# Mamba layer with a 16-state scan: the sum over the states as accumulating transposes

## The chip, the cores and the metric

One core of one Trainium2 chip. The metric is the device time in microseconds; three runs of the kernel before took 5519.04, 5524.55 and 5525.06 us, median 5524.55.

## The reference, cut to what matters

Two layers on x of shape (2, 512, 64, 64), each added to its input behind a group norm. Layer 0 is a Mamba block over 4096 tokens, 1024 inner channels and 16 states; layer 1 is linear attention with 8 heads. The change is in layer 0's scan:

```python
def step(h, inp):
    u_t, d_t, b_t, c_t = inp
    dA = jnp.exp(d_t[..., None] * A)
    dBu = (d_t * u_t)[..., None] * b_t[:, None, :]
    h = dA * h + dBu
    y = jnp.einsum('bdn,bn->bd', h, c_t)      # the sum over the 16 states
    return (h, y)
...
y = ys.transpose(1, 0, 2) + u * D_skip
y = y * jax.nn.silu(z)
out = y @ out_proj_w.T
```

## The kernel before, in words

All is f32. Layer 0 is cut into 16 chunks of 512 tokens (2 images x 8). A chunk has 8 tiles of 128 inner channels (j), a tile has 16 states (n), so a chunk has 128 slots, slot = 16 j + n. Every engine walks through the same slots in order, in a function of its own (scalar_chunk, vector_chunk, gpsimd_chunk, tensor_chunk, sync_chunk), and a table of slot numbers (lines 29 to 41) says in which slot it does what else. The loop over chunks runs with the scan of chunk c, the front part (norm, input projection, convolution, delta) of chunk c + 1, and the output projection of chunk c - 1 at once. Chunks 1 to 14 are one hardware loop (line 340), so each engine turns back 13 times.

A state (n) of a tile (j) goes through four engines:

- ScalarE, line 501: exp(delta * A) into one of three PSUM banks, two slots ahead; line 482: the last column of the previous scan is kept as the carry.
- VectorE, line 586: the product delta * u * B into one of eight hs buffers, one slot ahead; line 591: the scan.
- GpSimd, line 625: hc = h * C into one of four hc buffers, as soon as TensorE is done with the sum four states before (line 624).
- TensorE, line 718: y_ps += hc, a product with the identity as the weights and hc as the moving 128x512 operand, two slots behind (SUM_LAG). y_ps is one PSUM bank. The first of the 16 waits for y_skip (line 717), the last step's read of that bank.

Behind a tile's last sum, VectorE adds the skip term in slot 3 of the next tile (line 559, Y_SKIP), GpSimd multiplies with silu(z) in slot 5 (line 620, Y_GATE). In the same slots TensorE has the z products of the tile (line 692, slots 2, 2, 2, 3), the input products of the next chunk (line 660, four per inner tile, in slots 42 + 8 t to 45 + 8 t) and the output products of the chunk before (line 708). ScalarE has the group norm of the next chunk (line 398, slots 4, 5, 9, 10, the first waits for the load of xn), the copy of an input product out of PSUM (line 429, six slots behind its first part) with the last tap (line 435), and softplus (lines 457 to 472), whose Ln in slot 6 (10 for the last tile) brings a table load before it and one behind it. VectorE has the convolution (line 538). Each engine works strictly in the order of its code, so a wait holds up all that is behind it on that engine.

In layer 1 (from line 751) the same TensorE does plain f32 products of 128x128 (line 1047) and f32 transposes of 128x128 by the identity (line 1074).

```python
pe.wait_ge(hc_ready, step - SUM_LAG + 1)
if ns == 0:
    wait(pe, y_skip, tile)
pe.matmul(y_ps[:, :], identity[:, :], hc[:, ns % HC_RING, :], start=ns == 0,
          stop=ns == STATE - 1).then_inc(n_summed, 1)
```

Of the kernel before, what the change touches and what calls it, by code (L numbers as in the profile page):

```python
# [8 lines left out]
ACT = mybir.ActivationFunctionType  # L9
AX = mybir.AxisListType  # L10

P = 128
BATCH, DIM, TOKENS = 2, 512, 4096
CT = DIM // P
T = 512
CB = TOKENS // T
CHUNKS = BATCH * CB
INNER, STATE, TAPS, RANK = 1024, 16, 4, 32
# [4 lines left out]
GN_EPS = 1e-5  # L23
H_RING, HC_RING, DA_RING = 8, 4, 3
SUM_LAG = 2

# [9 lines left out]
DT_MM, SP_ABS, SP_EXP, SP_ROUND, SP_LN, SP_REST, SP_SUM, SP_DELTA = 14, 1, 3, 4, 6, 7, 9, 10  # L38
DT_MM7, SP_ABS7, SP_EXP7, SP_ROUND7, SP_LN7, SP_REST7, SP_SUM7, SP_DELTA7 = 3, 6, 7, 8, 9, 10, 11, 12
Z_MM, Z_TANH, Z_SILU = (2, 2, 2, 3), 8, 11  # L40
Y_SKIP, Y_GATE = 3, 5


def wait(engine, sem, value):

    if isinstance(value, int) and value <= 0:
        return
    engine.wait_ge(sem, value)
# [60 lines left out]
def mamba_and_linear_attention(nc, x, ln_w, ln_b, in_proj, conv_w, conv_b, x_proj, dt_proj, dt_b, a_log, d_skip,  # L109
# [9 lines left out]
    with outer:  # L119
# [3 lines left out]
        def sem(name):  # L123
            return outer.enter_context(nc.semaphore(name))

        identity = sb("identity", [P, P])
# [4 lines left out]
        with layer0:  # L131
# [30 lines left out]
            sp_l = sb("sp_l", [P, T], layer0)  # L162
# [3 lines left out]
            hc = sb("hc", [P, HC_RING, T], layer0)  # L166
# [4 lines left out]
            y_ps, da_ps = banks[0], banks[1:4]  # L171
# [139 lines left out]
            sp_sum = sem("sp_sum")  # L311
# [7 lines left out]
            h_ready = sem("h_ready")  # L319
            hc_ready = sem("hc_ready")  # L320
            n_summed = sem("n_summed")
            y_skip = sem("y_skip")
            gated = sem("gated")
            out_mm = sem("out_mm")
# [21 lines left out]
            with ExitStack() as main:  # L346
# [35 lines left out]
                def scalar_chunk(act, c, scan, front, project):  # L382
                    f = c + 1
                    for j in range(JT):
                        for n in range(STATE):
                            tile, slot = JT * c + j, STATE * j + n
# [63 lines left out]
                            if front if j == 7 else scan:  # L450
                                nt = tile + 1
                                dt_ps = pout if j == 7 else pb
                                jn = (j + 1) % JT
                                if n == (SP_ABS7 if j == 7 else SP_ABS):
                                    act.wait_ge(dt_mm, nt + 1)
                                    wait(act, delta_ready, nt)
                                    act.activation(sp_e[:, :], dt_ps[:, :], ACT.Abs,
                                                   bias=b_dt[:, jn:jn + 1]).then_inc(sp_exp, 1)
                                    act.activation(sp_m[:, :], dt_ps[:, :], ACT.Relu,  # L459
                                                   bias=b_dt[:, jn:jn + 1]).then_inc(dt_read, 1)  # L460
                                if n == (SP_EXP7 if j == 7 else SP_EXP):
                                    act.wait_ge(sp_exp, 2 * nt + 1)
                                    act.activation(sp_e[:, :], sp_e[:, :], ACT.Exp, scale=-1.0).then_inc(sp_exp, 1)
                                    act.wait_ge(sp_exp, 2 * nt + 2)
                                    act.activation(sp_w[:, :], sp_e[:, :], ACT.Identity,
                                                   bias=one[:, 0:1]).then_inc(sp_step, 1)
                                if n == (SP_ROUND7 if j == 7 else SP_ROUND):
                                    act.wait_ge(sp_step, 2 * nt + 1)
                                    act.activation(sp_w[:, :], sp_w[:, :], ACT.Identity,  # L469
                                                   bias=minus_one[:, 0:1]).then_inc(sp_step, 1)  # L470
                                if n == (SP_LN7 if j == 7 else SP_LN):
                                    act.activation(sp_l[:, :], sp_e[:, :], ACT.Ln, bias=one[:, 0:1]).then_inc(sp_ln, 1)  # L472
                            if scan and n == Z_TANH:
                                act.wait_ge(z_mm, tile + 1)
                                wait(act, gated, tile)
                                act.activation(zs[:, :], pb[:, :], ACT.Tanh).then_inc(tanh_z, 1)
# [27 lines left out]
                def vector_chunk(dve, c, scan, front, project):  # L504
                    f = c + 1
                    for j in range(JT):
                        for n in range(STATE):
# [47 lines left out]
                            if n == Y_SKIP and ((scan and j > 0) or (project and j == 0)):  # L555

                                jp, o = (j - 1) % JT, (c if j > 0 else c - 1)
                                dve.wait_ge(n_summed, STATE * tile)
                                dve.scalar_tensor_tensor(xs[:, o % 2, jp, :], xs[:, o % 2, jp, :], skip[:, jp:jp + 1],
                                                         y_ps[:, :], ALU.mult, ALU.add).then_inc(y_skip, 1)  # L560
                            if project and slot in OUT_ADD:
# [66 lines left out]
                def tensor_chunk(pe, c, scan, front, project):  # L628
                    f = c + 1
                    for j in range(JT):  # L630
                        for n in range(STATE):
# [80 lines left out]

                            if (scan and slot >= SUM_LAG) or (project and slot < SUM_LAG):
                                js, ns = (slot - SUM_LAG) // STATE % JT, (slot - SUM_LAG) % STATE
                                pe.wait_ge(hc_ready, step - SUM_LAG + 1)
                                if ns == 0:
                                    wait(pe, y_skip, tile)
                                pe.matmul(y_ps[:, :], identity[:, :], hc[:, ns % HC_RING, :], start=ns == 0,  # L718
                                          stop=ns == STATE - 1).then_inc(n_summed, 1)

                @block.sync
                def _(sp):
# [432 lines left out]
```

## Time and profile before

| | |
|---|---|
| median of 3 runs | 5524.55 us (5519.04 to 5525.06) |
| the profiled execution | 5522.59 us |
| its span in the trace | 5520.4 us |
| TensorE busy, whole span | 4475.3 us (81%), 10968 records |
| TensorE weight loads | 2016.5 us (37%) |
| VectorE busy | 4675.7 us (85%) |
| ScalarE busy | 3498.2 us (63%) |
| GpSimd busy | 3552.1 us (64%) |
| mean granted TensorE clock | 0.947 of full |

The shares are means over parts with different limits: layer 0's chunks fill about 170 to 4760 us of the span, layer 1 the rest. Busy time of TensorE is the union of records that overlap each other, so it says little on how full the engine is; the distance between the starts of records that follow each other does.

### The profile page before, as it was taken

To read this page: it belongs to the slowest core of one execution; us is meant where nothing else is said; L and a number is where in the kernel's file an instruction comes from. 1 tells how busy PE (TensorE), PEld (TensorE's weight loads), DVE (VectorE), ACT (ScalarE), POOL (GpSimd) and SP (SyncE) were. 2 spreads that over 40 slices of the span, in tenths; PEclk is the share of its full clock that TensorE was granted. 3 is DMA by queue.
4 is the path that set the end of the run, shared out by engine and by line. 5 is a ranking of instruction groups with operands and counts; after the bars stand their busy time and mean duration, and the time that the engine had idled before them with its cause. 6 is when DMAs were issued, how large, how long until landed. Compare 5 with 4: busy or idle time off the path is not lost. (4 is left out here: it accounts for less than half of the span.)

```text
span 5520.4 us, 58942 instructions
## 1 busy us (share of the span) xinstructions
PE 4475.3 (81%) x10968; PEld 2016.5 (37%) x10968; DVE 4675.7 (85%) x5565; ACT 3498.2 (63%) x6851; POOL 3552.1 (64%) x2778
## 2 busy tenths in 40 slices
PE   2788788888878787878787878887877887799998
PEld 0233233333333332323232323332323332486786
DVE  4899999999999999999999999999999999412212
ACT  1666666666666666666666666666666666464563
POOL 1577776777777777677777677776777778432422
PEclk9899999999999999999999999999999999999999
DMA  4102020202020202020201102020202020222313
GB/s 182 69 1 83 3 81 4 81 4 77 8 77 8 73 12 73 12 73 12 65 20 43 42 18 67 1 82 2 83 2 81 4 73 8 95 70 77 124 60 107
DMA packets 142648, 284.11 MB, mean 51 GB/s; under 512 B 13057, under 2 KB 14209, under 8 KB 140769
## 3 DMA queue, kind: packets, MB, share of 16 engines
q1 hardware_dynamic: 133856, 264.26, 15.2%
q10 hardware_dynamic: 8448, 16.78, 0.9%
q14 instruction: 312, 2.55, 0.1%
q8 instruction: 32, 0.52, 0.0%
HBM read 246.38 MB, written 34.60 MB: 51 GB/s over the span
## 5 line engine op out<-in xcount | busy, mean ns | idle before, releaser
L625 POOL TENSOR_TENSOR hc<-hs,bc 128x512 f32<-128x512 f32 x2048 | 2662.5, 1304 | 1285.5 <-DVE hs L591 1249.3
L718 PE MATMUL bank<-hc,identity 128*128 128x512 f32 x4096 | 2254.0, 644 | 723.0 <-POOL hc L625 614.4
L591 DVE TENSOR_TENSOR_SCAN hs<-bank,carry,hs 128x512 f32<-128x512 f32 x2048 | 2608.4, 1274 | 29.3 <-ACT bank L501 29.3
L718 PEld LDWEIGHTS bank<-hc,identity 128*128 128x128 f32 x4096 | 728.5, 196 | 2050.5 <-POOL hc L625 1437.0
L482 ACT ACTIVATE carry<-hs,keep_now 128x1 f32<-128x1 f32 x2032 | 588.6, 290 | 1338.9 <-DVE hs L591 1338.9
L586 DVE TENSOR_TENSOR hs<-bank,bc 128x512 f32<-128x512 f32 x2048 | 1376.8, 672 | 56.3 <-issue 48.8
L501 ACT ACTIVATE bank<-delta,neg_a 128x512 f32<-128x512 f32 x2048 | 1384.1, 676 | 58.7 <-DVE hs L591 55.3
L692 PE MATMUL bank<-xn,w_in 128*128 (+1 forms) x1024 | 533.4, 647 | 95.5 <-ACT sp_m L459 95.5
L660 PE MATMUL bank<-xn,w_in 128*128 (+1 forms) x1024 | 552.1, 626 | 18.6 <-ACT xn L422 10.8
L886 POOL TENSOR_TENSOR xg_low<-xg,xg_high 128x512 fp32r<-128x512 f32 x192 | 248.3, 1294 | 474.2 <-ACT xg_high L910 466.7
L708 PE MATMUL bank<-xs,w_out 128*128 (+1 forms) x1024 | 527.5, 604 | 2.8 <-DVE xres L566 2.8
L692 PEld LDWEIGHTS bank<-xn,w_in 128*128 128x128 f32 x1024 | 217.7, 214 | 390.2 <-issue 371.4
L660 PEld LDWEIGHTS bank<-xn,w_in 128*128 128x128 f32 x1024 | 207.0, 203 | 290.6 <-issue 266.2
L538 DVE SCALAR_TENSOR_TENSOR bank<-raw,w_conv,bank 128x512 f32<-128x512 f32 x384 | 287.1, 748 | 26.6 <-ACT bank L435 17.5
L708 PEld LDWEIGHTS bank<-xs,w_out 128*128 128x128 f32 x1024 | 197.1, 193 | 252.4 <-issue 236.3
L604 POOL TENSOR_TENSOR sp_w<-sp_w,sp_e 128x512 f32<-128x512 f32 x128 | 162.7, 1271 | 136.1 <-ACT sp_w L469 136.1
L910 ACT ACTIVATE xg<-xl,gn_bias,gn_scale 128x512 f32<-128x512 f32 x192 | 154.9, 807 | 137.4 <-DMA xl<-x 125.5
L999 DVE COPY ek_t<-l_bank 128x512 f32<-128x512 f32 x64 | 44.3, 692 | 219.2 <-PE l_bank L1074 219.2
L1004 DVE SCALAR_TENSOR_TENSOR keys<-l_bank,b_o,xl 128x512 f32<-128x512 f32 x64 | 48.0, 751 | 178.0 <-PE l_bank L821 178.0
L991 DVE TENSOR_REDUCE key_max<-keys 128x1 f32<-128x512 f32 (+1 forms) x64 | 42.3, 684 | 163.1 <-ACT keys L945 163.1
L614 POOL TENSOR_TENSOR delta<-sp_m,sp_w 128x512 f32<-128x512 f32 x128 | 168.3, 1315 | 0.1
L472 ACT ACT_TABLE_LOAD x128 | 164.2, 1283 | 2.3
(145 smaller groups left out, 4732.1 us busy)
## 6 DMA issues: line engine op xcount, KB each, us to landing
bc<-b_and_c_rows SPq DMA_DIRECT2D x512, 256.0 KB, 4.7
xl<-x SPq DMA_DIRECT2D x48, 1024.0 KB, 5.6
bc<-in_x SPq DMA_DIRECT2D x8, 2048.0 KB, 8.9
xn<-in_x ACTq DMA_DIRECT2D x16, 1024.0 KB, 7.6
xres<-in_x SPq DMA_DIRECT2D x64, 256.0 KB, 2.9
x<-xres SPq DMA_DIRECT2D x64, 256.0 KB, 2.0
out<-keys SPq DMA_DIRECT2D x16, 1024.0 KB, 5.0
w_in<-in_in_proj SPq DMA_DIRECT2D x1, 4096.0 KB, 12.7
```

Of the source, the lines that this page charges most:

```text
L482: act.activation(carry[:, col:col + 1], hs[:, (n - 1) % H_RING, T - 1:T], ACT.Copy, scale=keep_now[:, 0:1]).then_inc(carried, 1)
L501: act.activation(da_ps[target % STEPS % DA_RING][:, :], delta[:, jn % 2, :], ACT.Exp, scale=neg_a[:, jn, nn:nn + 1]).then_inc(da_ready, 1)
L538: dve.scalar_tensor_tensor(in_ps[t % 2][:, :], raw[:, TAPS - 1 - s:TAPS - 1 - s + T], w, in_ps[t % 2][:, :], ALU.mult, ALU.add).then_inc(c ...
L586: dve.tensor_tensor(hs[:, nn % H_RING, :], du_ps[:, :], bc[:, 0, nn, :], ALU.mult).then_inc(dbu_ready, 1)
L591: dve.tensor_tensor_scan(hs[:, n % H_RING, :], da_ps[slot % DA_RING][:, :], hs[:, n % H_RING, :], carry[:, STATE * j + n:STATE * j + n + 1 ...
L614: pool.tensor_tensor(delta[:, (j + 1) % 2, :], sp_m[:, :], sp_w[:, :], ALU.subtract).then_inc(delta_ready, 1)
L625: pool.tensor_tensor(hc[:, n % HC_RING, :], hs[:, n % H_RING, :], bc[:, 1, n, :], ALU.mult).then_inc(hc_ready, 1)
L660: mm = pe.matmul(in_ps[t % 2][:, :], w_in[:, ct, t * P:(t + 1) * P], xn[:, f % 2, ct, :], start=ct == 0, stop=ct == CT - 1)
L692: mm = pe.matmul(pb[:, :], w_in[:, ct, lo:lo + P], xn[:, c % 2, ct, :], start=ct == 0, stop=ct == CT - 1)
L708: mm = pe.matmul(out_ps[ct][:, :], w_out[:, k, ct * P:(ct + 1) * P], xs[:, o % 2, k, :], start=k == 0, stop=k == JT - 1)
L718: pe.matmul(y_ps[:, :], identity[:, :], hc[:, ns % HC_RING, :], start=ns == 0, stop=ns == STATE - 1).then_inc(n_summed, 1)
L886: pool.tensor_tensor(xg_parts[1][:, u, ct, :], xg[:, ct % 2, :], xg_parts[0][:, u, ct, :], ALU.subtract).then_inc(lowered, 1)
```

## The change

The sum over the states is made in another way. Per state, TensorE transposes the four 128x128 blocks of hc into the four column blocks of y_ps, all accumulating in that bank: the blocks of hc are the stationary operand and the identity (128 columns) the moving one. After the last state, y_ps holds the sum with channels and tokens exchanged within each block. ScalarE copies it into sp_l in slot 2 of the next tile (Y_COPY), and TensorE transposes the four blocks of sp_l back into y_ps, right behind the last sum in its code. The skip step waits for that (y_back) and moves to slot 4, the gate to slot 6. The Ln of softplus, which writes sp_l too, waits for y_back, and the copy waits for sp_sum, the last reader of sp_l.

```diff
+BLOCKS = T // P
...
-Y_SKIP, Y_GATE = 3, 5
+Y_COPY, Y_SKIP, Y_GATE = 2, 4, 6
...
                                 if n == (SP_LN7 if j == 7 else SP_LN):
+                                    wait(act, y_back, tile)
                                     act.activation(sp_l[:, :], sp_e[:, :], ACT.Ln, bias=one[:, 0:1]).then_inc(sp_ln, 1)
+                            if n == Y_COPY and ((scan and j > 0) or (project and j == 0)):
+                                act.wait_ge(n_summed, STATE * tile)
+                                act.wait_ge(sp_sum, tile)
+                                act.activation(sp_l[:, :], y_ps[:, :], ACT.Copy).then_inc(y_copied, 1)
...
                             if n == Y_SKIP and ((scan and j > 0) or (project and j == 0)):
-                                dve.wait_ge(n_summed, STATE * tile)
+                                dve.wait_ge(y_back, tile)
...
                                 if ns == 0:
                                     wait(pe, y_skip, tile)
-                                pe.matmul(y_ps[:, :], identity[:, :], hc[:, ns % HC_RING, :], start=ns == 0,
-                                          stop=ns == STATE - 1).then_inc(n_summed, 1)
+                                for q in range(BLOCKS):
+                                    mm = pe.matmul(y_ps[:, q * P:(q + 1) * P],
+                                                   hc[:, ns % HC_RING, q * P:(q + 1) * P], identity[:, :],
+                                                   start=ns == 0 and q == 0, stop=ns == STATE - 1,
+                                                   is_transpose=True, skip_group_check=True)
+                                mm.then_inc(n_summed, 1)
+                                if ns == STATE - 1:
+                                    pe.wait_ge(y_copied, tile)
+                                    for q in range(BLOCKS):
+                                        mm = pe.matmul(y_ps[:, q * P:(q + 1) * P],
+                                                       sp_l[:, q * P:(q + 1) * P], identity[:, :],
+                                                       start=q == 0, stop=True, is_transpose=True,
+                                                       skip_group_check=True)
+                                    mm.then_inc(y_back, 1)
```

## Rows read from the trace of the kernel before

**Rows 1.** Busy time by stretch, layer 0's chunks: engine, busy us (instructions), clock, DMA share, GB/s.
```profile
150.00:4740.00 4590.00, 3730.84 (x7686) 1451.38 (x7685) 4445.59 (x5194) 3062.07 (x6141) 3279.91 (x2560) 0.94 0.13 40
```

**Rows 2.** Groups of VectorE in that stretch: busy us, mean ns, idle before them, its end.
```profile
L591 DVE TENSOR_TENSOR_SCAN hs<-bank,carry,hs 128x512 f32<-128x512 f32 x2048 | 2608.4, 1274 | 29.3 <-ACT bank L501 29.3
L586 DVE TENSOR_TENSOR hs<-bank,bc 128x512 f32<-128x512 f32 x2048 | 1376.8, 672 | 56.3 <-issue 48.8 <-DVE bank L579 3.2
...
L559 DVE SCALAR_TENSOR_TENSOR xs<-xs,skip,bank 128x512 f32 (+1 forms) x128 | 92.5, 723 | 2.6 <-PE bank L718 2.6
```

**Rows 3.** ScalarE's wait for xn: whole span, then the shortest chunk (total us, times, longest).
```profile
ACT xn L398 <- DMA xn<-in_x: 22.8, 15, 4.6
...
ACT xn L398 <- DMA xn<-in_x: 0.2, 1, 0.2
```

**Rows 4.** The sums: their group, and their records (ns least, median, most).
```profile
L718 PE MATMUL bank<-hc,identity 128*128 128x512 f32 x4096 | 2254.0, 644 | 723.0 <-POOL hc L625 614.4 <-DVE xs L559 94.5
...
L718 PE MATMUL bank<-hc,identity x4096: 590/592/1223, 177.5 to 4730.3; 128*128 128x512 f32 x196
```

**Rows 5.** Timeline of TensorE in layer 1: start us, length us, line, count.
```profile
4887.40 0.60 PE L1074 MATMUL l_bank<-identity,ek 128*128 128x128 f32 x4
4887.83 1.06 PE L1047 MATMUL l_bank<-ek_t,v_t 128*128 128x128 f32 x8
```

**Rows 6.** Timeline at the start of an inner tile, ScalarE, TensorE and VectorE.
```profile
2111.93 0.68 ACT L501 ACTIVATE bank<-delta,neg_a 128x512 f32<-128x512 f32 x1
2113.33 0.30 ACT L482 ACTIVATE carry<-hs,keep_now 128x1 f32<-128x1 f32 x1 [0.72 <-DVE hs L591]
...
2113.56 2.74 PE L692 MATMUL bank<-xn,w_in 128*128 x6
...
2117.22 0.72 DVE L559 SCALAR_TENSOR_TENSOR xs<-xs,skip,bank 128x512 f32 x1
2117.86 0.68 DVE L586 TENSOR_TENSOR hs<-bank,bc 128x512 f32<-128x512 f32 x1
...
2119.66 0.67 DVE L586 TENSOR_TENSOR hs<-bank,bc 128x512 f32<-128x512 f32 x1
...
2121.60 1.02 PE L660 MATMUL bank<-xn,w_in 128*128 x2
2122.46 1.02 PE L718 MATMUL bank<-hc,identity 128*128 128x512 f32 x2
```

**Rows 7.** The same tile: the last input product, its copy by ScalarE, VectorE's convolution.
```profile
2123.32 1.02 PE L660 MATMUL bank<-xn,w_in 128*128 x2
...
2127.39 0.57 ACT L429 ACTIVATE raw<-bank 128x512 f32<-128x512 f32 x1
...
2128.38 0.75 ACT L435 ACTIVATE bank<-bank,b_conv,w_conv 128x512 f32<-128x512 f32 x1
...
2130.89 0.73 DVE L538 SCALAR_TENSOR_TENSOR bank<-raw,w_conv,bank 128x512 f32<-128x512 f32 x1
```

**Rows 8.** Busy time in stretches of 2 us before that tile; the third number from the end is the clock.
```profile
2109.00:2111.00 2.00, 1.99 (x2) 0.50 (x2) 2.00 (x3) 1.97 (x5) 1.17 (x1) 0.50 0.01 4
...
2113.00:2115.00 2.00, 2.00 (x6) 0.91 (x5) 1.93 (x4) 1.64 (x4) 1.27 (x1) 1.00 0.02 4
```

**Rows 9.** ScalarE's copy out of PSUM: ns least, median, most.
```profile
L429 ACT ACTIVATE raw<-bank x128: 572/575/597, 117.2 to 4431.3; 128x512 f32<-128x512 f32 x128
```

**Rows 10.** Timeline at the head of a chunk: z products, group norm, scan 8.
```profile
2187.19 4.65 PE L692 MATMUL bank<-xn,w_in 128*128 x6 [7.05 <-ACT sp_m L459]
...
2191.12 0.81 ACT L398 ACTIVATE xn<-xn,gn_bias,gn_scale  x1 [0.49 <-DMA xn<-in_x]
...
2199.07 1.28 DVE L591 TENSOR_TENSOR_SCAN hs<-bank,carry,hs 128x512 f32<-128x512 f32 x1 [1.83 <-ACT bank L501]
```

**Rows 11.** Timeline at the end of layer 0: last sums, output projection.
```profile
4728.51 2.35 PE L718 MATMUL bank<-hc,identity 128*128 128x512 f32 x4 [0.54 <-POOL hc L625]
4730.70 7.03 PE L708 MATMUL bank<-xs,w_out 128*128 128x512 f32 x16
```

More of the change, by code:

```diff
@@ L321, in mamba_and_linear_attention @@
             n_summed = sem("n_summed")
+            y_copied = sem("y_copied")
+            y_back = sem("y_back")
             y_skip = sem("y_skip")
```

## The prediction

> **What bounds the kernel now.** I first read the busy time per engine in the stretch that holds the sixteen chunks of layer 0 [rows 1]. VectorE is busy 4445.6 of 4590 us (97%), ScalarE 67%, GpSimd 71%. TensorE shows 81%, the figure that the change works on. Then the groups of VectorE and what their idle time waited for [rows 2]: the 2048 scans and 2048 products hold 3985 us, and of the waits only 2.6 us, once, were for TensorE (the last tile, behind the last scan). The others are 48.8 us at the 13 loop turns, where no other engine is waited for, and 29.3 us for ScalarE's exponentials. In the steady part VectorE goes from one product to the next in 1.80 us (2117.86 to 2119.66) [rows 6], whatever TensorE does. So the stretch is VectorE's work end to end, with one soft place: ScalarE at the head of a chunk. GpSimd's waits for a sum reach VectorE only through the ring of eight hs buffers, and none shows there.
>
> **The sums.** Removed: 2048 plain f32 products of 512 columns, two records each, 2254.0 us busy, 1.10 us each [rows 4]; back to back they start 0.86 us apart (2121.60, 2122.46) [rows 6]. Added: 2048 x 4 transposes of 128 columns. The nearest row is a group of four f32 transposes in layer 1: 0.60 us, and the next group starts 0.43 us after it (4887.40, 4887.83) [rows 5]. So some 2048 x 0.5 = 1020 us of TensorE time go. Bounds for one group of four: 0.43 us, and 1.06 us, the price of four plain 128x128 f32 products in two passes each [rows 5], if the chip ran the transposes so; even that is no dearer than today's sum. The sum of hc reaches PSUM about 0.4 us sooner, but nothing on VectorE waits for it, so this term is **0 us**. Its cover is VectorE's own work.
>
> **The copy and the way back.** Per tile ScalarE gets one 128x512 copy out of PSUM: 575 ns (raw<-bank) [rows 9], 128 x 0.6 = 77 us in all on an engine that is a third idle. In an inner tile it stands behind the exponential of 2111.93 to 2112.61, ends near 2113.2, and ScalarE idled until 2113.33 anyway [rows 6]: hidden. Behind the copy TensorE, which works in order, now stands still with its second group of four (0.4 to 0.7 us) and then the z products. They begin some 0.3 to 0.9 us later than 2113.56 and end near 2117.5. The result is wanted by VectorE's skip step, now at slot 4 behind 2119.66 instead of 2117.22 [rows 6]: 2 us of air. The Ln that now also waits for the second group comes at slot 6, later still. GpSimd's gate moves behind one more hc product; its reader, the tanh of z at slot 8, has several us left. What is queued behind TensorE's new wait are only these z products, and the first sum of the new tile, which waits for the skip step in either version.
>
> **The skip step one slot later.** It frees the one PSUM bank 1.8 us later. Behind it TensorE has three sums, three input products and one z product before the end of 2124.3 [rows 6, 7]. They cost 7 x 0.86 = 6.0 us, afterwards 4 x 0.86 + 3 x 0.43 = 4.7 us. So the input product ends 0.5 us later. Its reader, ScalarE's raw copy, starts at 2127.39, 3.0 us behind it [rows 7]: **0 us**. GpSimd wants a free hc buffer for state 4 only when scan 4 is done, over 1 us behind the first sum.
>
> **The head of a chunk.** Here VectorE does wait for ScalarE: 1.83 us at 2199.07, at the end of an unbroken run of ScalarE that starts when xn lands at 2191.12 [rows 10]. The copy falls ahead of that landing, and ScalarE idled 0.49 us there. Over the kernel that idle is 22.8 us in 15 places; the shortest is 0.2, three more lie at 0.4 and 0.5, all others above 0.6, and one chunk of sixteen has none [rows 3]. What exceeds the cover is 0.2 + 0.4 + 0.1 + 0.1 + 0.6 = **+1.4 us**. If nothing were covered it would be 16 x 0.6 = 9.6 us, the upper end; a gain is not excluded, should the landing come sooner, by at most a tenth of a us each.
>
> **The tail.** Behind the last scan TensorE starts the output projection at 4730.70, directly behind the last two sums, which ran at the lower clock (2.35 us for four records) [rows 11]. Everything up to layer 1 hangs on that projection. Now it also waits for a copy (0.6) and a second group (0.4 to 1.0), less what the last sum saves (0.4 to 0.6), and its first products may still find the lower clock. Bounds 0.4 and 4 us; I take **+2 us**, since the sums there already ran slow.
>
> **Sum.** 0 + 0 + 1.4 + 2 = +3.4 us. The profiled execution took 5522.6 us (span 5520.4), so 5526.0 in an execution like it. It lies 2.0 us under the median of the three runs (5524.55), so the forecast against that median is **5528 us**. 0.2% (11 us) is about what a measurement of this kernel can tell from no change.
>
> **TensorE's clock.** The granted clock stands at 0.50 from 2109 to 2111 us, 1.2 instead of 2.4 GHz, after some us in which TensorE did little but these sums; it is 1.00 again from 2113, when the sums at the low level had filled the engine and the input and z products follow [rows 8]. At the low level a record takes 1223 instead of 592 ns [rows 4]. After the change the same stretches hold half the work, so I expect the low level between the product bursts of every tile. A burst then pays until the clock is back: the three z products after an idle stretch took 4.65 us at 2187.19 against 2.74 us at 2113.56 [rows 6, 10], so about 1.9 us. That fits into the air counted above (2 us before the skip step, 3.0 us before raw). The Trainium skill, page TensorE: Matmul & The Clock Gate, section Part 4: PE-mode transpose, says that the full clock does not engage for transposes; no run here shows that yet. By that rule alone the transposes would give back no clock at all, and the sum would be that of the first rival.
>
> **Rivals.**
> 1. *Slower: the low clock lasts.* Place: tiles 3 to 6 of each chunk, where an input product must be done by slot 8. If everything behind the skip step ran at the low level, it would take 3 x 0.86 + 4 x 1.72 = 9.5 us and a slower last drain of 0.6 us, against 6.0 us today, and starts 1.8 us later: 5.9 us late. Cover is 3.0 us up to the raw copy, and between the end of the tap product on ScalarE (about 2129.1) and VectorE's convolution at 2130.89 another 1.8 us: 4.8 us [rows 7]. It decides from 4.8 us on, and costs 1.1 us x 4 tiles x 15 chunks = 66 us: **5594 us**. For it: the measured fall after thin work. Against: the clock came back within a burst each time. Partial forms (some tiles only) lie between 5535 and 5594. Chance 20%.
> 2. *Slower: ScalarE at the chunk head.* If the copy waits for a late last sum there, or the cover moves, 0.6 to 1.5 us a chunk, 10 to 24 us: **5545 us**. For it: the 29.3 us of waits all stem from there. Against: at the chunk's head TensorE had sat idle for 7.05 us, waiting for ScalarE, when its z products began at 2187.19, so the last sum was long done [rows 10]. Chance 8%.
> 3. *Faster: the loop turns and chunk heads shrink.* 48.8 us at 13 turns plus 29.3 us for ScalarE are the whole prize that is left [rows 2]; if lighter TensorE traffic took a third of the turns away: -16 us, **5508 us**. Nothing in the rows ties the turns to TensorE. Chance 6%.
> 4. *The transposes are not one pass each.* At 1.06 us a group the time is the forecast's; it is within that case.
>
> **How the numbers follow.** The forecast has 66%; its own range is 5516 to 5538 (bounds of head and tail, +0.4 to +14 us, and the 3 us by which executions differ). For 8 in 10, I add the lower partial forms of rival 1 and all of rival 2 above, and little below: 5512 to 5570. Faster by over 0.2%: 6% from rival 3, and 1% more. Slower by over 0.2%: 28% from rivals 1 and 2, less 2% for forms that cost under 11 us, and 1% from the upper edge of the forecast: 27%. The rest, 66%, is within 0.2%.
>
> **What would show it.** Right: TensorE's busy time in layer 0 falls by about 1000 us and the time does not follow; VectorE stays at 97%, with its scan at 1274 ns; the skip step shows no wait but the last; the granted clock of the stretch falls below 0.94, by how much I leave open; ScalarE is busy about 77 us more; the projection behind the last scan starts 1 to 4 us later. Wrong: VectorE's convolution or scans waiting for ScalarE by several us in tiles 3 to 6, ScalarE's raw copy waiting for TensorE (rival 1); the wait for ScalarE at slot 8 of a chunk at 2.4 us or more in most chunks (rival 2); loop turns under 3 us (rival 3); a group of four transposes above 1.1 us.

## The result, and the profile after

| | before | after |
|---|---|---|
| median | 5520.84 us (6 runs, 5518.59 to 5525.06) | 5544.44 us (6 runs, 5538.06 to 5546.35) |
| ratio | | 1.004, 95% interval 1.0028 to 1.0053 |
| profiled execution, its span | 5522.59, 5520.4 us | 5544.68, 5542.1 us |
| TensorE busy, mean granted clock | 4475.3 us, 0.947 | 4016.5 us, 0.83 |

The change costs 24 us by the medians and 22 us between the two profiled executions, twice what was called measurable. The forecast was 5528 us with 66% on "within 0.2%"; 5544 lies in the wide range (5512 to 5570), above the forecast's own (5516 to 5538).

The same stretch as in [rows 1], and VectorE's groups in it as in [rows 2]. Columns are as there. Line numbers are those of the new kernel: the scan is L599, the product of a state L594, the skip step L567.

```profile
150.00:4740.00 4590.00, 3250.64 (x12266) 1826.77 (x12265) 4443.11 (x5193) 3118.15 (x6268) 3284.41 (x2558) 0.81 0.14 41
```

```profile
L599 DVE TENSOR_TENSOR_SCAN hs<-bank,carry,hs 128x512 f32<-128x512 f32 x2048 | 2608.5, 1274 | 25.7 <-ACT bank L509 25.3
L594 DVE TENSOR_TENSOR hs<-bank,bc 128x512 f32<-128x512 f32 x2048 | 1376.5, 672 | 55.5 <-issue 47.9 <-DVE bank L587 3.2
...
L567 DVE SCALAR_TENSOR_TENSOR xs<-xs,skip,bank 128x512 f32 (+1 forms) x127 | 92.1, 725 | 7.8 <-PE bank L735 7.8
```

TensorE is 480 us less busy, not 1000: what runs beside the transposes now runs longer (clock 0.81 for 0.94). ScalarE is busy 56 us more. The scans are as long as before. The sums' own group, against [rows 4]:

```profile
L727 PE MATMUL bank<-identity,hc 128*128 128x128 f32 x8192 | 1456.9, 312 | 1076.1 <-POOL hc L633 977.7 <-issue 60.7 <-DVE xs L567 29.7
```

And the waits for the new steps and at the Newton product (slot 26, the first product of the step that refines the normalization's reciprocal square root), from the view of waits (total us, times, longest); the last line is the Newton product's wait in the kernel before:

```profile
ACT sp_l L480 <- PE bank L727: 43.1, 25, 3.4
...
DVE sq L525 <- ACT sq L418: 24.2, 15, 1.7
DVE xs L567 <- PE bank L735: 12.2, 14, 4.4
```

```profile
DVE sq L517 <- ACT sq L415: 15.5, 15, 1.0
```

**Where the 22 us sit.** In the two profiled executions: 2.0 us before the first scan, 10.1 between the first scan and the last, 3.7 from the last scan to layer 1, 5.9 in layer 1, whose code is the same. Counted from GpSimd's first instruction in it, layer 1 takes 757.0 us before and 762.9 after. It takes 757.8 to 759.5 us in the other kernels with plain sums and 759.0 with the transposes alone, but 758.7, 758.9, 761.9 and 762.8 in the four other versions of the change. The first scan starts anywhere from 168.3 to 173.3, and at 168.9 to 169.3 in those four. So the first part is a difference between executions; for layer 1 that is likely but not shown. The scan part and the tail are the change's.

VectorE's product for silu(z) runs once per tile, in slot 11. Cutting its work at the starts of these 128 records gives stretches from tile to tile; summed over the 16 chunks, against the kernel before:

```
us against before       tile 7 to 0   tile 0 to 1   the six others   all
after                      +4.0          +6.7            0.0        +10.7
```

In the six others not one stretch differs by over 0.1 us. All that the change costs among the scans, it costs in the two stretches around the head of a chunk, called the turn from here on. Cut finer, at the starts of the scans, it is +15.9 us up to the scan of slot 4, where VectorE waits 7.8 us for the way back and 4.5 us for the exponential of slot 3; then -11.7 up to slot 8, where the wait for ScalarE falls from 26.4 to 16.3 us; then -0.9 in slot 14 and +7.5 in slots 24 to 26. Of the last part, 4.5 us are at the Newton product: it waits 8.7 us more, but the products there then last 4.2 us less. A chain of small waits leads to it. The timeline of ScalarE in tile 1 of one chunk, first after, then before:

```profile
2223.57 0.68 ACT L509 ACTIVATE bank<-delta,neg_a 128x512 f32<-128x512 f32 x1
2226.41 0.60 ACT L480 ACTIVATE sp_l<-bank 128x512 f32<-128x512 f32 x1 [2.16 <-PE bank L727]
...
2227.70 0.62 ACT L466 ACTIVATE sp_e<-sp_e 128x512 f32<-128x512 f32 x1
```

```profile
2219.51 0.68 ACT L501 ACTIVATE bank<-delta,neg_a 128x512 f32<-128x512 f32 x1
2221.31 0.29 ACT L482 ACTIVATE carry<-hs,keep_now 128x1 f32<-128x1 f32 x1 [1.12 <-DVE hs L591]
...
2222.12 0.61 ACT L463 ACTIVATE sp_e<-sp_e 128x512 f32<-128x512 f32 x1
```

From the exponential to the next softplus step (2223.57 to 2227.70, before 2219.51 to 2222.12) ScalarE takes 4.13 us instead of 2.61, since it stands at the copy until the last sum has ended. The timeline of TensorE in the same place after the change, and the busy time by stretch (columns as in [rows 1]; the clock is the last but two):

```profile
2221.87 2.07 PE L654 MATMUL bank<-sq,channel_mean 128*128 128x512 f32 x2 [4.16 <-ACT sq L412]
2223.74 1.91 PE L716 MATMUL bank<-xs,w_out 128*128 x2
2225.44 0.93 PE L727 MATMUL bank<-identity,hc 128*128 128x128 f32 x4
```

```profile
2216.00:2218.00 2.00, 0.66 (x4) 0.42 (x4) 2.00 (x2) 0.56 (x1) 1.00 (x1) 1.00 0.00 0
...
2220.00:2222.00 2.00, 0.13 (x1) 0.13 (x1) 2.00 (x3) 1.61 (x4) 1.27 (x1) 0.50 0.01 4
...
2224.00:2226.00 2.00, 2.00 (x5) 0.86 (x5) 2.00 (x4) 0.25 (x1) 0.59 (x1) 0.50 0.34 131
2226.00:2228.00 2.00, 1.31 (x9) 0.81 (x8) 2.00 (x3) 1.59 (x4) 1.50 (x2) 0.98 0.43 115
```

TensorE had stood idle for 4.16 us, its clock had fallen to 0.50 (1.2 GHz), and a variance product (2.07 us), an output product (1.91) and the last sum run at that level one behind the other. Before, the same two products took 1.12 and 1.06 us, and the idle time ahead of them was 1.71 us. Over the kernel, the first record of the variance product in slot 17 ran at the low level (over 1 us instead of 0.70) in all 16 chunks, before in 3. What ScalarE loses here comes out eight slots later, where VectorE's Newton product waits 1.68 us instead of 1.04.

### The profile page after: what moved, and what is told of

Its sections match the earlier page's. It is cut to its first block and busy times, and to the rows that moved or that the text cites. A ratio compares the mean times of both kernels' runs of the same rounds, so it can differ in the third digit from the quotient of the medians.

```text
span 5542.1 us, 68442 instructions
## 1 busy us (share of the span) xinstructions
PE 4016.5 (72%) x15576; PEld 2403.1 (43%) x15576; DVE 4674.0 (84%) x5565; ACT 3555.2 (64%) x6979; POOL 3560.0 (64%) x2778
## 5 line engine op out<-in xcount | busy, mean ns | idle before, releaser
L599 DVE TENSOR_TENSOR_SCAN hs<-bank,carry,hs 128x512 f32<-128x512 f32 x2048 | 2608.5, 1274 | 25.7 <-ACT bank L509 25.3
L727 PE MATMUL bank<-identity,hc 128*128 128x128 f32 x8192 | 1456.9, 312 | 1076.1 <-POOL hc L633 977.7
L727 PEld LDWEIGHTS bank<-identity,hc 128*128 128x128 f32 x8192 | 1074.0, 159 | 2023.4 <-POOL hc L633 1486.3
L594 DVE TENSOR_TENSOR hs<-bank,bc 128x512 f32<-128x512 f32 x2048 | 1376.5, 672 | 55.5 <-issue 47.9
L700 PE MATMUL bank<-xn,w_in 128*128 (+1 forms) x1024 | 613.3, 732 | 11.2 <-ACT sp_m L462 11.2
L668 PE MATMUL bank<-xn,w_in 128*128 (+1 forms) x1024 | 605.7, 682 | 18.7 <-ACT xn L425 10.7
L716 PE MATMUL bank<-xs,w_out 128*128 (+1 forms) x1024 | 561.0, 639 | 4.7 <-DVE xres L574 2.9
L546 DVE SCALAR_TENSOR_TENSOR bank<-raw,w_conv,bank 128x512 f32<-128x512 f32 x384 | 287.1, 748 | 28.9 <-ACT bank L438 19.8
L735 PE MATMUL bank<-identity,sp_l 128*128 128x128 f32 x512 | 131.7, 406 | 181.5 <-ACT sp_l L480 181.5
L716 PEld LDWEIGHTS bank<-xs,w_out 128*128 128x128 f32 x1024 | 182.5, 204 | 103.4 <-issue 87.3
L735 PEld LDWEIGHTS bank<-identity,sp_l 128*128 128x128 f32 x512 | 84.4, 202 | 228.4 <-ACT sp_l L480 228.4
```

The costliest lines, as they stand in the source:

```text
L546: dve.scalar_tensor_tensor(in_ps[t % 2][:, :], raw[:, TAPS - 1 - s:TAPS - 1 - s + T], w, in_ps[t % 2][:, :], ALU.mult, ALU.add).then_inc(c ...
L594: dve.tensor_tensor(hs[:, nn % H_RING, :], du_ps[:, :], bc[:, 0, nn, :], ALU.mult).then_inc(dbu_ready, 1)
L599: dve.tensor_tensor_scan(hs[:, n % H_RING, :], da_ps[slot % DA_RING][:, :], hs[:, n % H_RING, :], carry[:, STATE * j + n:STATE * j + n + 1 ...
L668: mm = pe.matmul(in_ps[t % 2][:, :], w_in[:, ct, t * P:(t + 1) * P], xn[:, f % 2, ct, :], start=ct == 0, stop=ct == CT - 1)
L700: mm = pe.matmul(pb[:, :], w_in[:, ct, lo:lo + P], xn[:, c % 2, ct, :], start=ct == 0, stop=ct == CT - 1)
L716: mm = pe.matmul(out_ps[ct][:, :], w_out[:, k, ct * P:(ct + 1) * P], xs[:, o % 2, k, :], start=k == 0, stop=k == JT - 1)
```

## The experiments

Each was timed in five rounds beside the kernel before. "All" is the sum over the stretches as above. Most profiled executions lie within 5 us of their kernel's median, that of the copy alone 7 below and that of the one table 9 below, so an "all" is good to about that; the medians decide, the stretches say where.

**The parts of the change.** First the change in three parts, and pushed one slot further.

```diff
# later slots only, against before
-Y_SKIP, Y_GATE = 3, 5
+Y_SKIP, Y_GATE = 4, 6
# detour only: slots 2, 4, 6; plain sums, copy, way back as one plain product
# transposes only: the sums of the change, no copy, no way back, slots 3 and 5
# copy late, against the change
-Y_COPY, Y_SKIP, Y_GATE = 2, 4, 6
+Y_COPY, Y_SKIP, Y_GATE = 3, 5, 7
```

> Only the skip step and the gate are moved, to slots 4 and 6; plain sums, no copy. Three theories of where the 20 us of the change come from. A: the copy and the way back cost them by themselves, at ScalarE's two full stretches (slots 2 to 8 and 18 to 26 of a chunk) and in the tail. B: TensorE's lower clock costs them by itself. C: both are needed, the copy because it waits on ScalarE for a last sum that the low clock makes late. All three expect nothing here: 0 to +3 us, VectorE's waits in slot 26 at 1.04 us as before.

Measured: 5540.54 us, ratio 1.0035 (1.0021 to 1.0049) to 5518.73.

> The copy, the way back and the slots of the change, but plain sums of 512 columns and a plain product with the identity for the way back, so that TensorE is as busy as before. A: +14 to +20 us, the wait in slot 26 at 1.4 to 1.7 us, the skip step waiting at chunk heads. B: 0 to +3 us. C: +3 to +7 us, nearly all of it behind the last scan, clock 0.94 of full, slot 26 near 1.04 us.

Measured: 5539.09 us, ratio 1.0032 (1.0020 to 1.0044).

> The sums by accumulating transposes, without the copy and the way back (the skip step adds the sum with channels and tokens exchanged in each block, which this leaves as it is), skip and gate in slots 3 and 5. A: -1 to +1 us. B: +14 to +20 us. C: 0 to +3 us. All: the granted clock near 0.83 for the whole span, as after the change.

Measured: 5517.76 us, ratio 0.9995 (0.9987 to 1.0004). The sum stays with channels and tokens exchanged within each block, so the output is another one.

> The change with the copy, the skip step and the gate one slot later still: 3, 5, 7. A: the copy still stands ahead of the same work on ScalarE, so as the change, +18 to +26 us over before. B: the same as the change. C: the copy finds the last sum done, ScalarE's wait for it (43 us in 25 places after the change) falls below 10 us and the wait in slot 26 to near 1.1 us: 5 to 9 us under the change, +12 to +16 us over before, unless the first sum of a tile, now later, takes it back.

Measured: 5614.6 us, ratio 1.0165 (1.0150 to 1.0181).

All three theories fell with the first of these: the later slots alone, at a clock of 0.94, cost as much as the whole change, and the detour on top of them nothing. The third settles the clock by itself: 8192 transposes at this mean clock are free, though the variance product at the turn ran at the low level in 15 of 16 chunks. With the detour only, it did so in none, and the time is nearly that of the change. So the low clock is not shown to cost anything in the change.

```profile
150.00:4740.00 4590.00, 3237.73 (x11797) 1789.88 (x11796) 4442.77 (x5194) 3060.25 (x6137) 3278.58 (x2560) 0.80 0.13 41
```

The row is the busy time by stretch of the transposes alone. TensorE's busy time and the clock, 0.80, are those of the change, VectorE's busy time too, and the time is that of before. With the copy one slot later still, ScalarE's wait for the last sum falls to 3.5 us, as theory C said, but VectorE's waits at the Newton product stay at 24.9 us, and the time rises by 96 us. A new wait rules, ScalarE's tanh of z for the gate before it (view of waits):

```profile
ACT zs L484 <- POOL xs L628: 221.9, 116, 5.6
```

**Which of the two slots.**

```diff
-Y_SKIP, Y_GATE = 3, 5
+Y_SKIP, Y_GATE = 4, 5        # skip only; gate only: 3, 6
```

> The sums as before, with only the skip step in slot 4 (the gate stays in slot 5). Theory D (the order on GpSimd at the turn of a chunk): the extra time of the kernel with both moved comes from the gate. One slot later it stands against the denser list of tile 7, GpSimd's instructions then end 0.3 us later, and VectorE's products with two inputs in SBUF (delta times xs at the end of tile 7, the two Newton products in tile 0) fall beside another of GpSimd's instructions and are held. The skip step alone leaves the gate behind the same hc product, so 0 to +5 us against before, and delta times xs stays at 1.1 us in tile 7. Rival E (the bank): the skip step frees the one PSUM bank a slot later, the first sum of a tile comes 1.8 us later, and GpSimd waits for an hc buffer. Then this kernel alone shows the whole +18 to +20 us, and GpSimd's waits for a sum stand near the 198 us that the kernel with both moved showed, against 36 us before.

Measured: 5525.06 us, ratio 1.0008 (0.9999 to 1.0017).

> The sums as before, with only the gate in slot 6 (the skip step stays in slot 3). Theory D: nearly all of it, +12 to +20 us against before; delta times xs at the end of tile 7 is over 1.2 us in most chunks; GpSimd's waits for a sum stay near 36 us. Rival E (the bank): 0 to +3 us, since the bank is freed as before. If the two kernels share the loss or neither shows it, it takes both, and the place where GpSimd's lateness meets VectorE has to be read again.

Measured: 5520.65 us, ratio 1.0004 (0.9995 to 1.0013).

Neither shows it: each is within what can be told from no change, and only both together cost 20 us. Theory D had expected 12 us or more of the gate alone. Rival E falls plainly: with the skip step alone moved, GpSimd waited nearly five times as long for the sums as before (35.7 us), and it cost some 4 us, not 20. GpSimd's waits, with the skip step alone moved:

```profile
POOL hc L625 <- PE bank L718: 172.5, 162, 3.5
```

Theory D falls as to which slot, but the collision that it named is there where both are moved. VectorE's product delta times xs, once per tile, with two inputs in SBUF, lasts 0.68 us alone. With both moved it lasted 1.3 to 2.8 us at 12 of the turns (1.1 us before, and 1.1 us at nearly all of them with either one alone); here is one in VectorE's timeline, then GpSimd's of the same time:

```profile
1892.59 2.63 DVE L579 TENSOR_TENSOR bank<-delta,xs 128x512 f32<-128x512 f32 x1
```

```profile
1890.93 3.73 POOL L625 TENSOR_TENSOR hc<-hs,bc 128x512 f32<-128x512 f32 x3
1897.41 1.26 POOL L625 TENSOR_TENSOR hc<-hs,bc 128x512 f32<-128x512 f32 x1 [2.75 <-DVE hs L591]
```

GpSimd's run ends at 1894.66 and the product at 1895.22, 0.56 us later, as if it began only then. The Trainium skill, SBUF — State Buffer, section 🔬 SBUF: two separate sides, calls the port pair of the two engines an exclusive lock: of a VectorE instruction with two SBUF inputs and a GpSimd instruction that reads SBUF, whichever starts first has it for its whole length. These rows agree, in that the product ends only behind a GpSimd instruction. Over the kernel the held products are 9.3 us between two scans at the turn, against 0.7 us with the skip step alone. The stretch of the Newton products, which work on SBUF too, adds 5.0, but it adds 4.7 with the skip step alone as well; 6.6 are given back at the scan of slot 8, which waits for ScalarE that much less. In the change itself the product stays at 1.1 us, so this is not its path.

**The change in the old slots, and its Newton step later.**

```diff
-Y_COPY, Y_SKIP, Y_GATE = 2, 4, 6        # old slots
+Y_COPY, Y_SKIP, Y_GATE = 2, 3, 5
-RSTD, NEWTON, SCALE, AFFINE = 24, 26, 27, 29     # Newton later
+RSTD, NEWTON, SCALE, AFFINE = 24, 27, 28, 29
```

> The change with the skip step and the gate in their old slots, 3 and 5, and the copy still in slot 2. In inner tiles the way back ends near 2114.5, 2.7 us ahead of the old skip step, so nothing there. At the head of a chunk the way back ended 0.6 us after VectorE wanted it in slot 4, so in slot 3 VectorE waits about 2.4 us, 15 times, 36 us, and its later wait for ScalarE's exponential (about 0.9 to 1.8 us a chunk) goes for it. Theory D (the slots cost through GpSimd, the rest are sub-microsecond waits at the turn that stand for each other): waits of 30 to 36 us at the skip step, of which half are given back, so +10 to +20 us against before, the same as the change within 5 us. Rival F (the waits at the turn add up): +35 us or more against before, 15 us more than the change. Rival G (the later slots were the whole loss): 0 to +5 us.

Measured: 5555.71 us, ratio 1.0070 (1.0056 to 1.0083).

> The change with the product of the Newton step and its scaling one slot later (27 and 28). In the change VectorE waits there 1.68 us, 15 times, for ScalarE's second square, 0.65 us more than before, where ScalarE's new copy shifts what stands behind it. One slot later the operands are there. If that wait is on the path: the 24 us go, less what moves, so -15 to -24 us against the change, and 0 to +5 against before. If VectorE only meets ScalarE again at the next exponential: 0 to -5 us against the change.

Measured: 5541.63 us, ratio 1.0045 (1.0031 to 1.0058).

With the transposes alone at 5517.8, the copy and the way back in the old slots cost 38 us; the later slots save 12 to 16 of them. So in the change the later slots are a gain. In the old slots the skip step waits 50.5 us, and the scans wait 24 us less (VectorE's waits):

```profile
DVE xs L567 <- PE bank L735: 50.5, 31, 3.5
```

That is the time of rival F, 36 us above before, with half of the waiting given back, as theory D had it. The Newton step one slot later moves its wait and does not remove it: 2 us less than the change, as the second of the two expectations had it. The next scan meets ScalarE, which is still at the same unbroken run with four table loads of 1.28 us; its timeline, then VectorE's, with the Newton step later:

```profile
2234.99 1.28 ACT L416 ACT_TABLE_LOAD   x1
2236.28 0.69 ACT L416 ACTIVATE sq<-bank,eps 128x512 f32<-128x512 f32 x1
2236.99 1.28 ACT L418 ACT_TABLE_LOAD   x1
...
2239.48 0.68 ACT L509 ACTIVATE bank<-delta,neg_a 128x512 f32<-128x512 f32 x1
```

```profile
2240.19 1.28 DVE L599 TENSOR_TENSOR_SCAN hs<-bank,carry,hs 128x512 f32<-128x512 f32 x1 [2.34 <-ACT bank L509]
```

**Is it ScalarE's time?**

```diff
+                            if scan and n == Y_COPY:                # copy only, slot 2
+                                wait(act, sp_sum, tile + 1)
+                                act.activation(sp_l[:, :], delta[:, j % 2, :], ACT.Copy)
# one table: the block `if front and slot == RSTD` behind the Ln of slot 22,
# once in the kernel before, once in the change
-RSTD, NEWTON, SCALE, AFFINE = 24, 26, 27, 29
+RSTD, NEWTON, SCALE, AFFINE = 22, 26, 27, 29
```

> The kernel before, with one copy of 128x512 more on ScalarE in slot 2 of every tile (of delta, which nobody else waits for; its result is not used). No other order and no other wait is changed. Theory H (ScalarE is the second bound at two places of each chunk: up to the scan of slot 14 to 15 counted from the head, where VectorE waits 24.3 us in all for an exponential, and at the Newton product, where it waits 15.5 us): the 0.6 us come on top of these waits, 15 times at each, so +12 to +18 us; the waits read near 33 and 25 us. Rival (the loss of the change comes from TensorE's way back and from the later slots, not from ScalarE's time): 0 to +3 us, the waits where they were.

Measured: 5520.11 us, ratio 1.0002 (0.9993 to 1.0012).

> The kernel before, with ScalarE's Ln and Exp of the normalization moved from slot 24 to behind its Ln in slot 22, so that two of the four table loads of 1.28 us there fall away. Theory H: ScalarE is then 2.6 us ahead at the Newton product, VectorE's wait there (15.5 us) goes, so -10 to -18 us; the two Newton products vary by some us beside that. Rival I (VectorE meets ScalarE again at the next exponential, as in the change with the Newton step moved): 0 to -3 us.

Measured: 5531.2 us, ratio 1.0024 (1.0012 to 1.0036) to 5518.43.

> The change, with the same move of Ln and Exp. Theory H: its waits at the Newton product (24.2 us) and at the scan one slot ahead of it (2.1 us) go, so -20 to -28 us against the change, which is -6 to +4 us against before, while the skip step still waits 8 us at the head of a chunk. Rival I: as the change, +18 to +24 us against before.

Measured: 5560.39 us, ratio 1.0079 (1.0065 to 1.0093).

Theory H falls. (Its text puts the first wait at slot 14 to 15; by the trace it is at the scan of slot 8.) A copy of the same size in the same slot that waits for nobody is free, also at the turn: the Newton product waits as before. VectorE's waits with the copy alone:

```profile
DVE hs L594 <- ACT bank L504: 21.3, 17, 2.1
DVE sq L520 <- ACT sq L415: 15.7, 15, 1.1
```

So of the detour it is the waits that cost, not the 0.6 us. The move of Ln and Exp saves the Newton wait and pays 14.2 us two scans earlier, in slot 24, as ScalarE now reaches the variance sooner than TensorE has it. With plain sums it is 13 us slower than before, with the change 42, so neither theory H nor rival I holds. But it is a gauge of TensorE's lateness at this place. ScalarE's wait for the variance, with plain sums and with the change:

```profile
ACT sq L469 <- PE bank L646: 6.3, 4, 1.6
```

```profile
ACT sq L473 <- PE bank L654: 19.1, 15, 2.8
```

The stretch from tile 0 to 1 grows by 3.2 and by 28.9 us. The change makes TensorE late at the turn, with half the work in its sums. How much of that comes from the low clock and how much from TensorE's own wait for the copy, no run separates.

**A version that takes work from VectorE.** The rows said that the inner tiles are VectorE's alone and that a copy on ScalarE is free if it need not wait. So the copy takes over the skip step:

```diff
-Y_SKIP, Y_GATE = 3, 5
+Y_COPY, Y_GATE, W_SKIP = 2, 5, 14
...
+                                act.activation(xs[:, o % 2, jp, :], y_ps[:, :], ACT.Copy).then_inc(y_skip, 1)
...
+                                act.activation(w_skip, identity[:, :], ACT.Copy,
+                                               scale=skip[:, jn:jn + 1]).then_inc(w_skip_ready, 1)
...
+                                    pe.matmul(y_ps[:, :], w_skip, xs[:, c % 2, j, :], start=True,
+                                              stop=False).then_inc(skip_mm, 1)
```

> No transposes. The skip term is added by TensorE: ScalarE makes diag(skip) of a tile's 128 channels in slot 14 (128x128), TensorE multiplies it by xs as the first product of the tile's sum, and ScalarE's copy in slot 2 brings the finished sum from PSUM to xs; VectorE's skip step is gone, the gate stays in slot 5. VectorE's slot with the skip step is 0.66 us longer than without it (10.5 us in 16 tiles), so 128 x 0.66 = 84 us of the bound go. Against that stands the wait that the copy brings: ScalarE, in order, stands still in slot 2 until the last sum has ended. Theory J (what made the change slow is this wait where TensorE is late, at the turn of a chunk, and TensorE was late there because its clock had fallen to 0.50 in a stretch without work; the copy's own 0.6 us cost nothing): the sums here are plain and the clock stays near 0.94, so the wait at the Newton product stays at 1.0 to 1.2 us and the sum is -84 plus 0 to 15 us: 5435 to 5450 us. Rival K (the copy behind the last sum costs as much at full clock): -84 plus 20 to 40 us: 5455 to 5475 us, with the Newton wait at 1.6 us or more.

Measured: 5469.77 us, ratio 0.9916 (0.9903 to 0.9930) to 5515.82: 46 us faster than the kernel before, 70 faster than the change, each against the kernel before in its own rounds.

The six inner stretches behave as worked out, 10.6 us less each. The two of the turn don't: 12.8 us longer from tile 7 to 0, only 2.4 shorter from tile 0 to 1, so some 32 of the 84 us are lost there. VectorE's waits for exponentials rise from 29.3 to 51.5 us, while the Newton wait is 17.9. The time lies in rival K's range, but its sign, a Newton wait of 1.6 us or more, did not come: neither J nor K as written. A copy that waits seems to cost at the turn at full clock as well, but at the scans of slots 3 and 8 (13.8 and 31.4 us, before 0 and 26.4) rather than at the Newton product. It is not shown that the copy's wait does this: TensorE has one product more per tile here, and a faster VectorE meets the other engines sooner. ScalarE's waits for the last sum, and VectorE's for exponentials:

```profile
ACT xs L479 <- PE bank L727: 52.3, 84, 3.5
DVE hs L597 <- ACT bank L513: 51.5, 35, 2.1
```

All versions by stretch, from their profiled executions:

```
us against before       tile 7 to 0   0 to 1   1 to 2   2 to 7    all
later slots only           +4.0        +3.8     -0.2     +1.3     +8.8
skip only                  -1.5        +4.8     -0.1     +1.3     +4.6
gate only                  -3.4        +2.8     -0.1     -0.1     -0.8
detour only                +3.3        +7.7     -0.2     -0.6    +10.2
transposes only            -2.7        -2.7     -0.1     -0.5     -6.1
copy only                  -5.2        -1.2      0.0     -0.3     -6.7
one table                  -4.3        +3.2     -0.1     -0.4     -1.5
the change                 +4.0        +6.7      0.0      0.0    +10.7
 its Newton step later     +3.9       -24.6    +33.0     -0.1    +12.1
 in the old slots         +14.9       +12.3      0.0     -0.1    +27.1
 one table                 +2.5       +28.9     -0.1     -0.3    +31.0
 copy late                +25.5       +30.7     +9.6    +13.9    +79.8
skip on TensorE           +12.8        -2.4    -10.7    -53.3    -53.5
```

## Why the prediction was off by 16 us

- **What bounds the kernel: right.** VectorE's work is the bound, and TensorE's 480 us brought nothing; transposes alone give a ratio of 0.9995.
- **The sums, 0 us: right.** A group of four takes 0.60 us at full clock and starts every 0.43 us, as in layer 1; at 0.50 it takes 1.11. TensorE's busy time fell by 480 us, not by the 1000 of the prediction's sign, since the sums' own group fell by 797 and the rest ran longer at the lower clock.
- **The clock: right where it was looked at, and rival 1 (20%) did not happen.** Tiles 3 to 6 are unchanged to 0.1 us. Of the rule in the Trainium skill, TensorE: Matmul & The Clock Gate, Part 4: PE-mode transpose, that the full clock does not engage for transposes, the rows bear out a half. The clock fell in the idle time behind a group of transposes and was back at 0.98 from 2226 us, with other products about it, and the mean is 0.81; but three quarters of the 2048 groups took 0.60 to 0.68 us, so transposes do run at the full clock. In tile 1 of each chunk the clock has a part that was not looked for: ScalarE's copies there wait 32.2 us in 16 chunks with the change and 13.4 us with plain sums and the same detour. The two kernels' times differ by less than can be told, so that this costs anything is not shown.
- **The head of a chunk, +1.4 us: this is the step that failed.** It asked whether 0.6 us of copy fit into ScalarE's idle time, and they do (ratio 1.0002). What it left out is that the copy, in order, makes ScalarE wait for TensorE, 43.1 us in all, most of it in tile 1, and that VectorE has a second soft place there. The prediction named one, the scan of slot 8; the trace of before also has 15.5 us of waits for ScalarE at the Newton product. Between the scans the change measured +10.1 us, all of it at the turn.
- **The copy and the way back, "2 us of air": failed at the same place.** The air was read off an inner tile, where it holds. At the turn the way back comes too late, and the skip step waits 7.8 us in 13 of the chunks; the prediction's sign was that it waits only at the last.
- **The skip step one slot later, "0 us": wrong by itself, but not the path of the change.** Its reasoning, too, looked at inner tiles. The two later slots alone measured 20 us, though each alone measured 1 to 5 by the medians: each was priced against its own reader, and what they do together to the order in which VectorE and GpSimd meet at the turn stood in no term. In the change those held products are absent, and its later slots save 12 to 16 us against the old ones.
- **Rival 2 (8%) had the right mechanism,** a copy that waits for a late last sum, and the right time, 5545. The time is in part luck: the rival put it all at the head of a chunk, where the traces show 10 us, and its sign, a wait of 2.4 us at slot 8, did not come (1.1 us). The argument against it, that the last sum is long done, holds in tile 0 and was not made for tile 1.
- **The tail, +2 us:** 3.7 us. The last copy, the way back (1.11 us at the low level) and slower first projections, 9.03 us for sixteen records against 7.03 in [rows 11].
- **The forecast's own range does not follow from its terms.** The bounds of head and tail on 5524.55 give 5525 to 5539, with 3 us either way 5522 to 5542; the lower end of 5516 has no term behind it.

**What stays open.** Three versions cost 10 us among the scans at the same two stretches (+8.8, +10.2, +10.7) and 20 to 24 us by their medians, but through different rows: held products with the later slots alone; the skip step's wait for the way back (20.2 us, of which the scans' waits give back 19) with plain sums and the detour; Newton and skip waits with the change. That it is the turn is shown. Why these come out alike is not, nor is the part of the medians that the single profiled executions don't hold. With the later slots the detour adds nothing measurable (5540.5 and 5539.1), in the old ones it adds 38 us, so the parts' costs do not add up.

## What to carry to other kernels

Price a moved step at every stage of the loop, above all where the engines run level with each other (here the head of a chunk), not in the steady part alone. A step put on an idle engine costs what that engine must now wait for, with all that stands behind it in order; its own length may be free. And where one engine's work fills the time, change another's load only if it takes something off the first: half of the work in TensorE's sums was worth nothing, 0.66 us of VectorE per tile was worth 46 us.

## What the runs showed of the hardware

- f32 transposes that accumulate into one PSUM bank over 16 states work, four blocks in 0.43 us from start to start, half of the 0.86 us of one plain 128x512 product.
- The clock fell to 0.50 within an idle time of 4.16 us of TensorE in this place (1.00 from 2216 to 2218 us, 0.50 from 2220), though the engine had run through an idle time of 1.71 us in the same place before at 1.00.
- VectorE's product with two SBUF inputs was held beyond a boundary between two GpSimd instructions (2.63 us beside a run of three). That happened at 4 of the 15 turns with both slots moved; at the other turns the product went in at the first boundary, and GpSimd's instruction behind it then took some 1.7 us instead of 1.26. A lock that goes to whoever comes first would not have made one expect the four.
